# Product-key weight groups in eight halves, one 64-column matmul per token half, the two f16 planes added by VectorE

## What is computed

```python
sim = jnp.einsum('pbnhd,hkpd->pbnhk', q, keys)
s, i = jax.lax.top_k(sim, k)
all_scores = (sx[..., :, None] + sy[..., None, :]).reshape(b, n, h, k * k)
all_idx = (ix[..., :, None] * nk + iy[..., None, :]).reshape(b, n, h, k * k)
scores, pk = jax.lax.top_k(all_scores, k)
idx = jnp.take_along_axis(all_idx, pk, axis=-1)
o = jnp.einsum('bnd,bnhkd->bnhk', inputs, w_down)
o = jax.nn.gelu(o, approximate=False) * jax.nn.softmax(scores, axis=-1)
return jnp.einsum('bnhk,bnhkd->bnd', o, w_up)
```

## Time and profile before

| | |
|---|---|
| median of 3 runs | 2983.77 us (2981.38, 2983.77, 2987.13) |
| profiled execution, span from first to last instruction | 2977.3 us |
| its own time | not given apart; the three runs lie 4.1 to 9.8 us above the span |
| PE busy | 2840.2 us (95%) |
| DVE busy | 1919.1 us (64%) |
| ACT busy | 1215.2 us (41%) |
| POOL busy | 491.4 us (17%) |
| L989 PE, the groups, 8192 matmuls | busy 123.9 us |
| L998 DVE, 128 multiplications of G | busy 151.6 us |

### The profile page before, as it was taken

How to read it: one execution, slowest core, us unless ns; L and a number is a source line. 1 busy time by engine, 2 the same in 40 slices (tenths; PEclk the granted TensorE clock), 3 DMA queues, 4 the chain that set the end, 5 groups by cost and what they waited for, 6 DMA issues and landing times.

```text
span 2977.3 us, 72660 instructions
## 1 busy us (share of the span) xinstructions
PE 2840.2 (95%) x28558; PEld 2187.9 (73%) x28558; DVE 1919.1 (64%) x6577; ACT 1215.2 (41%) x2721; POOL 491.4 (17%) x616
## 2 busy tenths in 40 slices
PE   8999979999999999999999999978999859999998
PEld 4895467777777777777777777645676639999998
DVE  4553587777777777777777777466777654444443
ACT  2332232333334343434343333235555525555554
POOL 0555400000000000000000000012334313333333
PEclk9999989999999999999999999999999979999999
DMA  3552300101010000101010101111222232222222
GB/s 141 175 158 82 140 2 23 33 23 34 23 34 30 26 32 25 36 24 34 23 34 23 33 23 33 37 36 41 70 77 63 59 121 33 37 37 40 37 37 33
DMA packets 94322, 148.90 MB, mean 50 GB/s; under 512 B 20048, under 2 KB 76240, under 8 KB 90896
## 3 DMA queue, kind: packets, MB, share of 16 engines
q1 hardware_dynamic: 73728, 107.83, 11.0%
q0 software_dynamic: 20112, 36.40, 6.0%
q10 hardware_dynamic: 144, 0.03, 0.0%
HBM read 95.93 MB, written 48.27 MB: 48 GB/s over the span
## 4 chain that ended last, share of the span: by engine, by line
PE 87%; DVE 6%; DMA 2%; ACT 2%; issue 2%; SPq 0%; POOL 0%; POOLq 0%; DVEq 0%; ACTq 0%
PE ps L1008 16%; PE ps L827 15%; PE ps L2075 9%; PE ps L1077 8%; PE ps L2090 8%; PE ps L1044 4%; PE ps L989 4%; PE ps L420 2%; PE ps L431 2%; PE ps L857 2%; PE ps L858 2%; PE ps L1560 2%; PE ps L1516 1%; PE ps L266 1%; PE ps L267 1%
## 5 line engine op out<-in xcount | busy, mean ns | idle before, releaser
L827 PEld LDWEIGHTS ps<-arena 128*128 128x128 f32 x4096 | 536.4, 192 | 29.1 <-issue 2.9
L1008 PE MATMUL ps<-arena 128*128 128x256 f32 x2048 | 550.7, 392 | 3.0 <-DVE arena L998 2.0
L827 PE MATMUL ps<-arena 128*128 128x128 f32 x4096 | 538.9, 276 | 0.9 <-ACT arena L835 0.9
L1008 PEld LDWEIGHTS ps<-arena 128*128 128x128 f32 x2048 | 354.7, 190 | 164.1 <-issue 132.9
L835 ACT ACTIVATE arena<-ps 128x256 f32<-128x256 f32 x512 | 196.0, 383 | 546.4 <-PE ps L827 545.9
L1077 PE MATMUL ps<-arena 128*16 128x256 f32 x4096 | 270.6, 382 | 8.4 <-DVE arena L1107 7.6
L2075 PE MATMUL ps<-arena 128*128 128x128 f32 x2272 | 265.4, 275 | 0.1
L1803 POOL MEMSET arena<- 128x3072 f32 x1 | 2.7, 2658 | 1569.6 <-PE ps L1008 1569.6
L2075 PEld LDWEIGHTS ps<-arena 128*128 128x128 f32 x2272 | 259.4, 192 | 0.4 <-issue 0.3
L2090 PE MATMUL ps<-arena 128*128 128x256 f32 x1136 | 256.8, 379 | 0.0
L1098 DVE SCALAR_TENSOR_TENSOR arena<-arena 128x128 f32<-128x128 f32 x256 | 73.7, 288 | 280.6 <-ACT arena L1089 280.6
(11 more groups left out here) (287 smaller groups left out, 4631.3 us busy)
## 6 DMA issues: line engine op xcount, KB each, us to landing
xw_scratch<-arena SPq DMA_DIRECT2D x32, 512.0 KB, 2.7
arena<-xw_scratch SPq DMA_DIRECT2D x256, 64.0 KB, 2.7
arena<-in_W SPq DMA_DIRECT2D x16, 1024.0 KB, 5.2
ys_scratch<-arena SPq DMA_DIRECT2D x71, 128.0 KB, 1.8
xn_scratch<-arena SPq DMA_DIRECT2D x32, 129.0 KB, 3.0
arena<-in_xT SPq DMA_DIRECT2D x8, 512.0 KB, 8.1
arena<-in_kinT SPq DMA_DIRECT2D x8, 512.0 KB
arena<-in_xtb SPq DMA_DIRECT2D x32, 128.0 KB, 2.2
```

Of the source, the lines that this page charges most:

```text
L827: m = e.matmul(bank(b)[:, 128 * i:128 * i + 128], kin[:, k, 2 * jp + i, :], xcT[:, k, 128 * blk:128 * blk + 128], start=(k == 0), stop=(k ...
L1008: m = e.matmul(bank(7)[:, 0:256], G[blk % 2][:, j, :], kout[:, j, :], start=(j == 0), stop=(j == 31))
```

## The change

Each group of 16 tokens is cut into two halves of 8 tokens (u = 0 to 7 in a block). For a token one matmul has both planes as 64 moving columns and adds nothing in PSUM, so the two planes come out side by side. ScalarE copies the second plane of a half to SBUF (`wcopy_scalar`, L1004 of the changed kernel), VectorE adds the first plane (`wsum_vector`, L1008) and multiplies G by the sum (`wgroup_vector`, L1015). Half u stands at the head of slot u on all three engines. Some of the top-k's operations move on VectorE within their slots or by a slot, `onehot_vector` for group 0 of the next block goes from slot 7 to slot 6, the SBUF arena is 2048 words larger, and the scratch of the software DMA is set to 8192 bytes.

```diff
-    WORDS = 53200
+    WORDS = 55248
...
+        wt = [take(2, 8, 32) for _ in range(2)]
...
-                e.wait_ge(s["wg"], n - 1)
+                e.wait_ge(s["wg"], 2 * n - 2)
...
-        def wgroup_tensor(e, blk, r):
-            b, n = r % 2, 4 * blk + r
-            e.wait_ge(s["xy"], 3 * n + 3)
+        def planes(i):
+            return bank(4, 2).rearrange("p (g t i j) -> p g t i j", g=2, i=2, j=32)[:, :, :, i]
+
+        def wgroup_tensor(e, blk, u):
+            b, n, t0 = u // 2 % 2, 8 * blk + u, 8 * (u % 2)
+            if u % 2 == 0:
+                e.wait_ge(s["xy"], 3 * (4 * blk + u // 2) + 3)
             if n:
-                e.wait_ge(s["A"], n)
-            for q in range(16):
-                for i in range(2):
-                    for half in range(2):
-                        p0 = 64 * half
-                        m = e.matmul(bank(4 + half)[:, 32 * q:32 * q + 32], X[b][p0:p0 + 64, q // 2, :, q % 2],
-                                     Y12[b][p0:p0 + 64, i, q // 2, :, q % 2], start=(i == 0), stop=(i == 1))
+                e.wait_ge(s["wt"], n)
+            for q in range(8):
+                t = t0 + q
+                for half in range(2):
+                    p0 = 64 * half
+                    m = e.matmul(bank(4 + half)[:, 64 * q:64 * q + 64].rearrange("p (i j) -> p i j", i=2),
+                                 X[b][p0:p0 + 64, t // 2, :, t % 2], Y12[b][p0:p0 + 64, :, t // 2, :, t % 2],
+                                 start=True, stop=True)
             m.then_inc(s["wg"], 1)
 
-        def wgroup_vector(e, blk, r):
-            n = 4 * blk + r
-            gv = G[blk % 2].rearrange("p j (g t) -> p g j t", g=2)[:, :, :, 16 * r:16 * r + 16]
+        def wcopy_scalar(e, blk, u):
+            n = 8 * blk + u
             e.wait_ge(s["wg"], n + 1)
+            if n >= 2:
+                e.wait_ge(s["A"], n - 1)
+            e.activation(wt[u % 2], planes(1), ACT.Copy).then_inc(s["wc"], 1)
+
+        def wsum_vector(e, blk, u):
+            e.wait_ge(s["wc"], 8 * blk + u + 1)
+            e.tensor_tensor(wt[u % 2], planes(0), wt[u % 2], ALU.add).then_inc(s["wt"], 1)
+
+        def wgroup_vector(e, blk, u):
+            t0 = 8 * u
+            gv = G[blk % 2].rearrange("p j (g t) -> p g j t", g=2)[:, :, :, t0:t0 + 8]
+            e.wait_ge(s["wt"], 8 * blk + u + 1)
             e.wait_ge(s["G"], 16 * blk + 16)
-            e.tensor_tensor(gv, gv, bank(4, 2).rearrange("p (g t j) -> p g j t", g=2, j=32), ALU.mult).then_inc(s["A"], 1)
+            e.tensor_tensor(gv, gv, wt[u % 2].rearrange("p g t j -> p g j t"), ALU.mult).then_inc(s["A"], 1)
...
                     if jp % 2 == 0:
+                        if mid:
+                            wgroup_tensor(e, i + 1, jp // 2)
                         for t in step_of(i, jp // 2):
                             step_tensor(e, t)
...
-                    if mid and jp % 4 == 1:
-                        wgroup_tensor(e, i + 1, jp // 4)
...
                 for k in range(8):
+                    if mid:
+                        wcopy_scalar(e, i + 1, k)
                     for t in step_of(i, k):
                         gates_scalar(e, t)
...
                 for k in range(8):
+                    if mid:
+                        wsum_vector(e, i + 1, k)
+                        wgroup_vector(e, i + 1, k)
                     for t in step_of(i, k):
                         cell_vector(e, t)
                     if more:
                         if k == 0:
                             best2_vector(e, i + 2, 0, 4)
-                        elif k == 1:
-                            split_vector(e, i + 2)
...
-                        if k == 5 or k == 6:
-                            place_vector(e, i + 3, 4 * k - 20, 4 * k - 18)
+                        if k == 6:
+                            place_vector(e, i + 3, 9, 11)
                         elif k == 7:
+                            place_vector(e, i + 3, 14, 16)
                             pairs_vector(e, i + 3)
                     for t in step_of(i, k):
                         hidden_vector(e, t)
-                    if mid and k % 2:
-                        wgroup_vector(e, i + 1, k // 2)
                     if i >= 0 and k == 7:
                         x1_vector(e, i)
                     if mid and k in (1, 3, 5):
                         onehot_vector(e, i + 1, k // 2 + 1)
+                    if more and k == 6:
+                        onehot_vector(e, i + 2, 0)
...
+                        elif k == 1:
+                            split_vector(e, i + 2)
...
                         if k == 4:
                             best_vector(e, i + 3, 0, 8)
                             best_vector(e, i + 3, 8, 16)
+                            place_vector(e, i + 3, 0, 4)
                         elif k == 5:
-                            place_vector(e, i + 3, 2, 4)
+                            place_vector(e, i + 3, 4, 9)
                         elif k == 6:
-                            place_vector(e, i + 3, 6, 16)
-                    if more and k == 7:
-                        onehot_vector(e, i + 2, 0)
+                            place_vector(e, i + 3, 11, 14)
...
-    nc = bacc.Bacc("TRN2", target_bir_lowering=False, num_devices=1)
+    nc = bacc.Bacc("TRN2", target_bir_lowering=False, num_devices=1, dynamic_dma_scratch_size=8192)
```

More of the change, by code:

```diff
@@ L1001, in outmm_tensor @@
             if jp == 0:
-                e.wait_ge(s["A"], 4 * blk + 4)
+                e.wait_ge(s["A"], 8 * blk + 8)
                 if blk == 0:
@@ L1183, in peer_scalar @@
             for i in range(-2, NBLK):
-                past, more, next_ = i >= 1, i + 2 < NBLK, i + 3 < NBLK
+                past, mid, more, next_ = i >= 1, 0 <= i + 1 < NBLK, i + 2 < NBLK, i + 3 < NBLK
                 for k in range(8):
+                    if mid:
+                        wcopy_scalar(e, i + 1, k)
                     for t in step_of(i, k):
```

## The result

The changed kernel takes 3091.81 us (median of 4 runs, 3088.59 to 3095.78) against 2982.57 us for the kernel before in the same series. The ratio is 1.0368, 95% interval 1.0354 to 1.0383: slower by 109 us, where 50 were forecast, and outside the range. The sign and the two closed chains of the forecast are there; the size is not, and a third wait came that the forecast had excluded.

A forecast was written before the change was run, and what follows sets the result against it. TensorE's own work bounds the kernel. A block: -0.96 saved, +1.01 and +1.23 waits, +1.28 us; 37 in steady blocks and 12 at edges on 2977.3 make 3026, plus 6.5 to median: 3033 us; 3003 to 3060 (8 in 10).

The forecast's parts named there:

- the two closed chains: Loops from half group to half group through ScalarE and VectorE; TensorE waits 1.01 us before slot 6, 1.23 before slot 4.
- third wait: Excluded by the forecast: outside slots 1, 3 and 5 the LSTM's result, at 3.7 us plus up to 1, comes before 5.03.
- What bounds the kernel: Steady block of 48.73 us: TensorE's own work sets the time, VectorE has 12.4 us of slack.
- What TensorE saves: Half groups of 0.33 us (0.30 to 0.35), eight taking 2.64 instead of 3.60 us: 0.96 us saved a block.
- The rival of the halves: Partition halves run one after the other with 64 columns, half groups take 0.52 us: 3071 us, chance 0.07.
- Copy and sum: ScalarE's eight copies a block take 0.60 us each, VectorE's eight sums 0.69 each, plus 0.03 of waiting.
- The multiplication: VectorE's product of G and the sum, eight of 512 elements a block: 0.61 us each, 0.82 at worst.
- Slots 0, 1, 2, 4 and 7: No TensorE waits there; slot 1 has 0.7 us to spare, the others need only the LSTM's result before 5.03.
- one of my signs of being wrong about the rest of VectorE's order: TensorE idle time in slots 0, 2, 4, 6 or 7 would show the forecast wrong about VectorE's remaining order.
- The edges: First and last blocks of the part, i = -1, 0, 29 and 30: together +12 us.
- Memory: Larger arena moves addresses only, smaller DMA scratch taken as nothing; rival that scratch holds GpSimd's queue up: chance 0.03.
- From span to median: The runs' median lies 6.5 us above the profiled span, so 3026 us of span becomes 3033 us.

The follow-up runs named there:

- e2: Changed kernel with wt stored in the order of G, so the multiplication reads SBUF word after word; 3044.89 us, ratio 1.0218.
- e3: Changed kernel without ScalarE's copy and the sum, the multiplication reading the first plane from PSUM; 3001.08 us in one run.
- e5: Kernel before, its own 64-matmul groups moved to the head of TensorE's slots, next block's group 0 one-hots to slot 6; 3113.8 us, ratio 1.0434.
- e9: Changed kernel with wt in G's order, half groups ending slots, sum and multiplication one slot later, next block's one-hots split, transposes later; 2992.47 us, ratio 1.0035.
- e1: Kernel before with only the larger arena (55248 words) and the software DMA scratch of 8192 bytes; 2979.4 us, ratio 0.9998.

## Why the prediction was wrong

- *What bounds the kernel*: right. TensorE's own order set the time. In slot 5 the chain grew beyond TensorE's work, and the slot with it, from 5.04 to 6.46 us.
- *What TensorE saves*: right in kind. A half group takes 0.35 us of the chain, my upper end, so 0.80 us a block instead of 0.96. The halves of the partitions run side by side with 64 columns too: the records of 16 matmuls run for 0.41 us, one lasts 0.19, so 15 starts take 0.22, 14.7 ns each, where one after the other would need 27. The rival of the halves falls. A pair went from 25.3 to 29 ns. The one spacing for 1 to 64 columns in the table that the Trainium skill gives in "TensorE: Matmul & The Clock Gate", section "Back-to-back issue gap", does not hold here at 64: it would have made 0.29 us. The formula above that table, columns over 2.4 plus 2.5, makes 29.2 ns for 64, which is what each half shows.
- *Copy and sum*: right, 0.60 and 0.69.
- *The multiplication*: **the step that failed.** I took 0.61 us for 512 elements out of a row that reads PSUM, and 0.82 as the worst. The changed one reads SBUF across its order and costs 0.98 in the queue, 1.07 by itself. In two chains that is +0.74 us a block, and the third wait of 0.63, which I had excluded (the LSTM's result "before 5.03"), came from it. e2 takes all of that away: with nothing but this operand's order mended the time is 3044.89 us, 12 above my 3033 and inside my range. Its block of 50.03 beside the forecast 48.73 + 1.28 = 50.01 is closer than the terms deserve: the saving was 0.16 smaller, and the wait of slot 3 is 0.84 where I had 1.23.
- *The closed chains of slots 3 and 5*: right in place and form. The waits are 1.20 and 1.35 against 1.23 and 1.01, but with the multiplication 0.37 longer than I took. With e2's they are 0.84 and 0.98, so slot 5 was sized right and slot 3 some 0.4 too large. I had TensorE arrive at +8.82 there; it comes later, because without the group of 0.90 ahead of them the transposes of slot 3 are reached before `rows_vector` ends. They start 1.19 us after the gelu matmuls in front of them (1270.93 to 1272.12) and before the change 0.89 (1261.14 to 1262.03).
- *Slots 0, 1, 2, 4 and 7*: no waits for one-hots, as forecast; but slot 0 has the wait of 0.63 for the LSTM's result, and idle time there was one of my signs of being wrong about the rest of VectorE's order.
- *The edges*: wrong, 39 us (20.9, 14.2 and 4.2) against some 15 (the 12, and two steady blocks of 1.28 that lie in the 14.2). At the start I counted the added work of VectorE once (+6) and little for waits; e3, without copy and sum, loses 11.6 there, e5, which adds no work, 11.9, and e9, with both, only 2.5. So it is the place that costs at the start too, where there is no LSTM and the slots are shorter. The last 4.2 us come with the clock's later return, and may be no more than the spread of one kernel.
- *Memory*: right, nothing (e1).
- *From span to median*: I added 6.5 us, and here the median lies 0.7 above the profiled span. The runs lie about 2 us above their own spans; the rest was the draw of the profiled execution.

With 0.98 for the multiplication in the forecast's own sum, a block would have been +1.28 + 0.16 + 0.74 and, with the third wait as measured, + 0.6: 2.8, beside the 2.76 measured. Slot 3, 0.4 too large in my sum, and the short wait before the transposes, which it does not have, are in that agreement too.

## What to carry to other kernels

When work that one engine feeds to the next is moved to the head of a slot, follow the whole loop from that instruction to the next one that waits for it: e5 adds nothing and loses 130 us, because what was read a slot late is now read at once. Price a moved operand by its own memory and order: a tensor read transposed from PSUM for nothing is not free once it lies in SBUF; write it transposed instead. And where a queue is 88% full (45.3 of 51.4 us), 0.4 us more in each of its operations can delay a result slots later, so look for the third wait after the two that you found. It is the place that decides: e9's VectorE is 86% full (42.0 of 48.6), and its block is no longer than before.

## What was not expected of the hardware

- VectorE's product of two f32 operands of 512 elements, one read from SBUF with 128 or 132 bytes between neighbours: 1.07 and 1.08 us; in order: 0.69. From PSUM with 64 words between neighbours, the sum took 0.69 us and ScalarE's copy 0.60, as in order.
- The output matmuls right behind f16 half groups took 1.06 us of the chain, as they do behind the LSTM's step, instead of 0.87 behind gelu matmuls.
- In e5, where TensorE is idle for 3.1 us of a block, the granted clock fell below 1.00 for moments in the steady part (means of 0.91 to 0.96 in ten stretches of 20 us); in the changed kernel, idle for 3.3 us of a block, it did not. No run tells why.
- Executions of one kernel, the one before, differ by 7.6 us in span, with a mean granted clock from 0.981 to 0.986. A part whose instructions did not change took 4 us more in the changed kernel's trace, with a mean clock of 0.87 instead of 0.96 in 40 us of it; the 40 us ahead had 0.83 in both.
